# Two recurrent layers on one core: the second layer's router and value products stream 128 columns instead of 8 or 16

## The reference, cut to what matters

```python
xn = _layernorm(x, axis=-1)
s = _L1_attn_ref(xn, WQ, WK, WV)                       # plain causal attention
g = _silu(_L1_ffn_ref(xn, ...))                        # what follows here
x = x + s * g

# inside _L1_ffn_ref
x = x + _attention(_rmsnorm(x, w_ln1), Wq, Wkva, Wkvb, Wo)   # 16 heads
ckv = x @ Wkva                                         # first 16 columns: latent (R = 16)
kv = (kv_latent @ Wkvb) ...                            # keys without rotation, and the values
...
logits = xf @ Wgate + expert_bias                      # 8 experts
probs = softmax(logits); top-2, normalised
routed = sum over experts of comb * experts(xf)
```

## Time and profile before

| what | value |
|---|---|
| median of 3 runs | 1393.14 us (1389.89 to 1395.06) |
| profiled execution | 1388.76 us, span 1386.9 us |
| mean granted TensorE clock | 0.885 |
| PE busy | 1198.3 us, 86% of the span |
| PEld busy | 724.8 us, 52% |
| DVE busy | 988.6 us, 71% |
| ACT busy | 654.2 us, 47% |
| POOL busy | 285.5 us, 21% |

### The profile page before, as it was taken

One profiled execution on the slowest core, in us unless ns is written; L12 is line 12 of the kernel. 1 busy time (PEld: TensorE's weight loads), 2 busy tenths in 40 slices (PEclk: granted clock), 3 DMA queues, 4 the chain that ended last, 5 costly groups with the idle time before them and its releaser, 6 DMA issues.

```text
span 1386.9 us, 21579 instructions
## 1 busy us (share of the span) xinstructions
PE 1198.3 (86%) x7497; PEld 724.8 (52%) x7497; DVE 988.6 (71%) x1636; ACT 654.2 (47%) x1306; POOL 285.5 (21%) x363
## 2 busy tenths in 40 slices
PE   7589989897458988998999999999989999999844
PEld 6478878796124434535444544544554464453332
DVE  6758868797567777976987897888798776454222
ACT  3658667664325335355445435545444523533411
POOL 1085345440303103202100410320230200000000
PEclk9589999998767689899989989988998998997867
DMA  7499878884352333243253235315324301300101
GB/s 209 139 310 303 279 254 277 269 275 154 99 115 85 92 93 105 85 92 98 85 115 103 90 92 119 112 61 114 94 93 104 88 25 32 62 25 10 47 16 38
DMA packets 99526, 168.38 MB, mean 121 GB/s; under 512 B 25973, under 2 KB 53469, under 8 KB 99357
## 3 DMA queue, kind: packets, MB, share of 16 engines
q1 hardware_dynamic: 76636, 90.98, 24.2%
q0 software_dynamic: 22784, 76.04, 17.5%
HBM read 142.68 MB, written 11.17 MB: 111 GB/s over the span
## 4 chain that ended last, share of the span: by engine, by line
PE 48%; DVE 12%; DMA 5%; ACT 5%; issue 4%; POOL 1%; SPq 1%; POOLq 0%; DVEq 0%; ACTq 0%
PE bank L1197 11%; PE bank L1215 4%; PE bank L1232 4%; PE bank L1200 3%; PE bank L1392 3%; PE bank L1235 3%; PE bank L1262 3%; PE bank L1266 3%; PE bank L1296 2%; DMA rec_wide<-head_recips 2%; PE bank L1253 2%; ACT probs L1407 2%; DVE neg_max L1562 1%; PE bank L1384 1%; DVE sc_state L298 1%
## 5 line engine op out<-in xcount | busy, mean ns | idle before, releaser
L1562 DVE TENSOR_REDUCE neg_max<-bank 128x2 f32<-128x1024 f32 (+3 forms) x256 | 203.8, 817 | 159.4 <-PE bank L1235 159.2
L1407 ACT ACTIVATE probs<-bank 128x1024 f32<-128x1024 f32 (+1 forms) x192 | 168.9, 880 | 300.6 <-PE bank L1200 300.3
L1197 PE MATMUL bank<-q_all,kk 49*128 49x512 f32 (+3 forms) x1024 | 224.7, 517 | 23.3 <-ACT probs L1407 18.4
L212 POOL DMA_DIRECT2D sc_bc_wide<-scan_bc x128 | 73.2, 572 | 510.3 <-DVE sc_ub L291 261.9
L298 DVE TENSOR_TENSOR_SCAN sc_state<-sc_a,sc_ub 128x1024 f32<-128x1024 f32 x64 | 145.9, 2280 | 0.1
L764 PE MATMUL bank<-xcol,wst 128*128 128x128 f32 x1152 | 143.7, 279 | 1.7 <-DMA wst<-bias_cols 1.7
L764 PEld LDWEIGHTS bank<-xcol,wst 128*128 128x128 f32 x1152 | 137.1, 195 | 2.9 <-DMA wst<-bias_cols 2.9
L1197 PEld LDWEIGHTS bank<-q_all,kk 49*128 49x128 f32 x1024 | 81.7, 195 | 103.8 <-issue 48.3
L1232 PE MATMUL bank<-kr,q_all 48*128 48x512 f32 (+3 forms) x512 | 113.3, 439 | 23.5 <-DVE neg_max L1562 17.6
L883 POOL DMA_INDIRECT xrow<-sorted_in,token_of x72 | 94.1, 1307 | 150.5 <-PE bank L755 104.6
L906 DVE SCALAR_TENSOR_TENSOR hid<-bank,wst,gel 128x128 f32<-128x128 f32 x288 | 80.3, 340 | 41.6 <-issue 40.0
(11 more groups left out here) (274 smaller groups left out, 1845.0 us busy)
## 6 DMA issues: line engine op xcount, KB each, us to landing
sc_bc_wide<-scan_bc POOLq DMA_DIRECT2D x128, 512.0 KB, 5.1
wst<-in_wexp SPq DMA_DIRECT2D x72, 512.0 KB
q_all<-q_kind SPq DMA_DIRECT2D x96, 128.0 KB, 4.4
rec_wide<-head_recips SPq DMA_DIRECT2D x32, 256.0 KB
p_t<-gates_turned SPq DMA_DIRECT2D x16, 512.0 KB, 6.4
sorted_out<-xrow SPq DMA_DIRECT2D x8, 576.0 KB, 6.4
rows_all<-in_x SPq DMA_DIRECT2D x8, 256.0 KB, 4.1
sorted_in<-rows_all SPq DMA_DIRECT2D x8, 256.0 KB, 5.8
```

The source lines that it names most:

```text
L1197: mm(bank[1][:, par, at:at + n], kk[rows, b % 2, kt * P:(kt + 1) * P], q_all[rows, quad // 2 % 3, pair, kt * P:L].bitcast(F32), start=True ...
L1407: af(probs[:, slot % RING, :, 0:width], bank[1][:, :, 0:width], ACT.Exp, scale=0.125).then_inc(s["p_ready"], 1)
L1562: last = v.tensor_reduce(neg_max[:, quad % 2, i, pr:4:2], bank[0][:, :, at:at + (i + 1) * P], AX, ALU.max, negate=True)
```

## The change: what it does, and the diff

The moving operand of both products becomes a view of the same 8 or 16 columns, repeated with stride 0 until it has 128 columns. The stationary operands, the number of instructions, the order, the waits and the semaphores stay. Each chunk's result now takes 128 columns of the bank: 16 copies of the 8 logits, or 8 copies of the 16 latents. The readers take the first copy of each chunk.

```diff
@@ router, TensorE
-  last = mm(to[:, j * E:(j + 1) * E], xm_t[:, j * P:(j + 1) * P], c["router1"][:], start=True, stop=True)
+  last = mm(to[:, j * P:(j + 1) * P], xm_t[:, j * P:(j + 1) * P], c["router1"][:].unsqueeze(1).to_broadcast([P, P // E, E]), start=True, stop=True)
@@ values, TensorE
-  last = mm(to[:, j * LAT:(j + 1) * LAT], xr_t[:, j * P:(j + 1) * P], c["wlat"][:], start=True, stop=True)
+  last = mm(to[:, j * P:(j + 1) * P], xr_t[:, j * P:(j + 1) * P], c["wlat"][:].unsqueeze(1).to_broadcast([P, P // LAT, LAT]), start=True, stop=True)
@@ values, ScalarE
-  af(vaug[:, b % 2, :, 0:LAT], bk(5)[:, 0:J * LAT].rearrange("p (j f) -> p j f", j=J), ACT.Copy).then_inc(s["vaug_ready"], 1)
+  af(vaug[:, b % 2, :, 0:LAT], bk(5).rearrange("p (j f) -> p j f", j=J)[:, :, 0:LAT], ACT.Copy).then_inc(s["vaug_ready"], 1)
@@ router, VectorE
-  v.tensor_tensor(prob[:], bk(7)[:, 0:J * E].rearrange("p (j e) -> p j e", j=J),
+  v.tensor_tensor(prob[:], bk(7).rearrange("p (j e) -> p j e", j=J)[:, :, 0:E],
```

## The result

| | before | changed |
|---|---|---|
| median of 14 runs each | 1392.86 us | 1385.87 us |
| ratio, 95% interval | | 0.9942 (0.9915 to 0.9968) |
| profiled execution, span | 1386.9 us | 1376.9 us |
| mean granted TensorE clock | 0.885 | 0.905 |
| PE busy | 1198.3 us | 1174.9 us |

Two later comparisons of the same changed kernel on other chips gave 0.9887 (0.9856 to 0.9918) and 0.9873 (0.9828 to 0.9918). So the change makes the kernel faster by 0.6 to 1.3%. Forecast were 12 us (0.9%). The first comparison's medians differ by 7.0 us, and its interval ends at 11.8; 12 us lie inside the intervals of the two later ones.

A forecast was written before the change was run, and what follows sets the result against it. PE at half clock in eight stretches was taken as the bound, DVE close behind, so DVE's waits were the gain: 7.55 + 3.7 + 3.0 + 0.5 = 14.75, less 0.4, less a sixth: 12 us, median 1381 us, range 1367 to 1393.

The forecast's parts named there:

- the stretch from 1166: Half-clock stretch from 1166.1: DVE waits 5.34 us for PE there, of which 3.7 us were to be won.
- The lump sixth taken off: Whole sum, 14.3 to 12 us: for a shifted pipeline, PE's standstill behind L1215, and row loads and head reciprocals.
- The products' own price: Router and values products on PE: 0.02 to 0.05 us more per group, 16 groups, taken as 0.4 us.
- The stretch from 818: Half-clock stretch from 818.0: DVE's waits for PE of 0.54 and 1.49 us counted as gain, 2.03 us.
- The stretch from 477: Behind block 1's values: clock falls before them, returns from about 480; 3.0 of 4.68 us of DVE's waits won.
- The stretch from 1268: Behind block 6's router, no values following: clock expected to fall a little later all the same, 0.5 us won.
- Either the clock does not fall at a router, or it falls and comes back sooner: Behind the routers: with 128 columns either no fall, or the clock returns some 3 to 7 us sooner.
- The argument on the clock: Around block 0's router: columns streamed keep the clock, not being busy (2.85 of 3.4 us against 1.83 of 3.2).
- the first (falls all the same): Rival: transposes, wait and gaps around the router cause the fall; +0.4 to -3 us; chance 0.22 with the fourth.
- the slow operand: Rival at both products: stride-0 reads restart, 1.73 us per group, 11 us slower, 1404 us; chance 0.06 with other losses.
- The second (more than DVE's waits): Rival: clock also holds from 1268.3 and L1562's waits shorten; 20, up to 25 us won; chance 0.12.
- The fourth (the copies do not raise what the clock is judged by): Rival: copies are written but the clock's level is judged otherwise; the first rival's time; chance 0.22 with the first.

The follow-up runs named there:

- filler_in_wait: Kernel before, both products narrow, plus one 128 x 512 product nobody reads in PE's wait ahead of each router: 1383.03 us, 0.9951.
- values_32: Kernel before with the values product streaming 32 columns (two copies of 16), router still 8: 1394.44 us, 1.0008.
- values_only: Kernel before with only the values widened to 128 columns, router left at 8: 1372.43 us, 0.989.
- hole_filled: Changed kernel plus two 128 x 512 products nobody reads in PE's wait ahead of slot 36's maxima: 1386.78 us, 0.9908 to the kernel before.
- queries_first: Changed kernel with the query products L1253 moved ahead of the maxima in the same slot: 1389.62 us, 0.992 to the kernel before.
- before_again: The kernel before, unchanged, repeated for a second profile: 1390.06 us, 1.0001.
- router_only: Kernel before with only the router widened to 128 columns, values left at 16: 1383.59 us, 0.9922.
- contiguous: Changed kernel with the 128 columns as real copies laid out on the host, no stride 0: 1379.08 us, 0.9903 to the kernel before.
- both_third: The changed kernel, both products wide, repeated a third time: 1376.3 us, 0.9873 to the kernel before.

## Why the prediction was right, step by step

**The mechanism held.** PE's clock fell behind the routers because few columns streamed, and columns put back kept it: filler_in_wait shows it from one side (five routers of six), values_32 from the other. The gain was DVE's waits for PE and not PE's halved time: shown by the floor of 25.9 us that values_only, hole_filled and queries_first all reach by different ways, with L1577 at the same 15.2 us. Stretch by stretch, in the first pair of profiles (router slots, before minus changed):

| stretch from | 477 | 585 | 701 | 818 | 937 | 1053 | 1166 | 1268 | sum |
|---|---|---|---|---|---|---|---|---|---|
| forecast, us | 3.0 | 1.15 | 2.29 | 2.03 | 0.67 | 1.41 | 3.7 | 0.5 | 14.75 |
| measured, us | 0.6 | 1.8 | 2.2 | -1.1 | 0.6 | 1.1 | 3.6 | 2.7 | 11.5 |

Of the 11.5 us, 1.3 went to a later first exponential (425.6 against 424.3 us) and 0.2 to the other slots, which leaves the span's 10.0. Five of the eight terms are within 0.7 us. One of the five is luck: before_again had no fall in the stretch from 1166 and needs 24.0 us there, as the changed kernel does, with nothing widened. Against before_again the eight terms sum to 8.5 us. The lump sixth taken off was not worked out either, so that the sum fits (11.5 against 12) says less than the single terms.

**What was mis-sized.**
- *The products' own price.* I took 0.02 to 0.05 us per group, from the ends of the records. The row taken as the measure, 1.05 us with 128 real columns, was right for the values (L1328 above), but those take 0.96 us with 16 columns at full clock (router_only), not 1.03. The router's groups are 1.13 us instead of 1.03, and from the router's start to the next scores' start it is 1.05 us instead of 0.96 (702.35 to 703.40; before, 700.20 to 701.16). That is 0.1 us a group, 1.6 us for the 16, not 0.4, if all of it counted. The Trainium skill's isolated gap (page "TensorE: Matmul & The Clock Gate", section "Back-to-back issue gap") would have given an estimate of 4 us; the trace lies between.
- *The stretch from 818.* The forecast named PE's new standstill behind L1215 as a hole and took a lump sixth off for it and two other things. It is the largest loss, -1.1 us instead of 2.03: in the changed kernel and its repeats PE waits 1.8 us for L1562 and L1253 then runs at half clock in most blocks, mostly 0.7 to 1.0 us each against the floor, and 2 to 8 us where the scan's output delays it too (k = 3: 31.7, 35.7 and 29.7 us against 27.8).
- *The stretch from 477.* 0.6 us instead of 3.0, though the clock came back as forecast, at 479.9. The forecast had 1.70 us of it as DVE's wait for L1253. But DVE also waits there for the transfers of the first query tile (L1101). With L1253 done at 484.75, the last of them landed at 486.75, and L1577 began right behind it:

```profile
482.81 1.94 PE L1253 MATMUL bank<-xr_t,wq_kind 128*128 128x512 f32 x4
...
486.83 0.69 DVE L1577 TENSOR_TENSOR q_kind<-bank,cos_q 128x512 f32<-128x512 f32 x1 [2.00 <-issue]
```

  In the kernel before they had landed at 484.68, while PE was still at L1253. Counted from slot 10's exponential L1577 starts at 14.89 us instead of 15.52: 0.6 us sooner. PE ran ahead and waited 1.54 us for DVE in front of L1232 (491.83), and the clock fell again at 493.6.
- *The stretch from 1268.* I expected 0.5 since the clock would fall again. It did, from 1265.0, but for 10.2 us and not 20.5: 2.7 us.

**What it missed in kind.** "Either the clock does not fall at a router, or it falls and comes back sooner" were put down as equals. They are not. A fall of 3.4 us beside DVE's top-two chain costs nothing that can be seen (25.9 us with it in values_only, and 25.9 in hole_filled where nothing falls); a clock held through it lets PE run into a wait, and the fall comes where PE is needed. The router's half of the change is therefore worth nothing once the values are wide.

**A reading that was unlike.** The argument on the clock set PE's 2.85 busy us of 3.4 before the fall against 1.83 of 3.2 before a rise. The second number is L1392 alone. All of PE is busy for 2.63 of these 3.2 us, 82% against 84%. So the two rows hardly differ in PE's busy share, and the argument has less force than the prediction gave it. That the columns count was a guess at that point; values_32 and filler_in_wait made it a finding.

Of the rivals, the first (falls all the same) and the slow operand are out: by the windows and by contiguous. The second (more than DVE's waits) didn't come about in the first result; 0.9873 in both_third would be 18 us, but in its profile the other slots were shorter by 4 us too, and nothing shows that this is the change's. The fourth (the copies do not raise what the clock is judged by) is out as well: they kept it.

**Still open:** why the other slots differ by up to 15 us between executions of nearly the same program. The half-clock stretches in them move from profile to profile, and no experiment held them still. The 19 slots from 39 on, around block 1's end, vary most: seven of the twelve later profiles are 1 to 9 us longer there than the two of before, the four of one chip most, and part of that is the wait that no row explains. Open too is why the clock fell over L1253 in most blocks of the changed kernel but not in k = 1, with the same wait of 1.8 us ahead of it.

## What to carry to other kernels

Before an engine's slow stretch is priced, look at who waits for it there: the gain came out of the 18 us that DVE waited for PE there (7.55 + 5.34 + 4.68 by the forecast's own terms), and not out of the 47 us by which, as an estimate (half of 94.7), the half clock stretched PE's busy time. In those seven stretches the changed kernel is 8.8 us shorter than before, 5.2 of them against before_again, and values_only 15.5. Before a wait is counted as gain, look for what else ends just behind it: in the stretch from 477 a transfer let only 0.6 of 1.70 us come back. Eight instructions with 8 or 16 moving columns take here nearly the time of eight with 128 (1.03 against 1.13 us, 0.96 against 1.05), and the clock fell behind all seven routers between blocks (six of them in before_again), at the first though PE was busy 2.85 of 3.4 us. Where such a product lies inside a half-clock stretch, widening it with copies is nearly free (0.1 us per eight instructions) and brought the clock back after 3.4 us instead of 10.2 and more. Where the clock may fall for free is worth knowing as well: the hole beside DVE's top-two chain did no harm, and closing it pushed the fall to where it did.

## What the runs showed of the hardware

- A moving operand read with stride 0 streams like a contiguous one: 1.13 us for a router's group in the changed kernel and in contiguous.
- Eight loads with products of 128 columns take 0.1 us longer than with 8 or 16 columns at full clock; the distance between starts is the same, 0.11 us, apart from the first (0.18 us for the router, where it was 0.10). At half clock a values group takes 1.92 us instead of 1.73, 0.21 us between starts either way.
- A wait of PE of only 1.8 us, between dense work on both sides, was followed by a fall to 1.2 GHz in most blocks (712.0, 824.6, 944.1 and 1056.7 in the changed kernel) and not in others (590.65). With the wait filled (hole_filled) it did not come in k = 2, 4 and 5. The Trainium skill (page "TensorE: Matmul & The Clock Gate", section "HAM oscillation — how this bites in real kernels") describes a clock that falls again and again for waits on DMA. By these traces a short wait for another engine does the same.
- Products that nobody reads keep the clock too: 3.84 us for 32 instructions behind 10.6 us of them, 5.29 to 6.60 behind a wait of 12 us. Behind 2.06 us of wait after the last filler it fell all the same.
